# Sums of exponentials of two head groups: from TensorE products with ones to GpSimd additions

## The chip, the cores and the metric

One core of a Trainium2 chip runs the whole program in one launch. The time is the device time of an execution in microseconds (us); the figure for a kernel is the median of its runs. The engines are TensorE (PE), VectorE (DVE), ScalarE (ACT), GpSimd (POOL), and SyncE (SP), whose queue issues most transfers.

## The reference

Two layers over x of 8 x 112 x 512 with a context of 8 x 375 x 512: an attention without projections, a feed-forward with ternary weights, a second attention with projections, and a last feed-forward with integer weights. The change lies in the second attention, which is, for 16 heads of 32:

```
q = hs @ Wq.T + bq ; k = ctx @ Wk.T + bk ; v = ctx @ Wv.T + bv
scores = clip(q k^T / sqrt(32), -50, 50), -10000 where masked, clipped again to -50
probs  = softmax(scores) over the 375 context tokens
delta  = clip(residual_scale, 0, 0.3) * ((probs @ v) @ Wo.T + bo)
x      = x + layernorm(delta) * gamma + beta
```

The softmax is computed as exp(score) and a division by the sum over tokens afterwards. This sum, one number per element, head and query row, is what the change computes in another way.

## The kernel before

The program is written by hand for each engine, with semaphores; no scheduler moves anything, so each engine works in the order in which the code of its block stands.

Stages in order of time: first attention with the key and value projections of the context beside it (to about 135 us), ternary feed-forward (to about 240 us), query projection (to about 266 us), second attention (266 to 370 us), last feed-forward (to the end).

The second attention runs over 8 batch elements (`b`) and in each over G = 4 groups of 4 heads (`g`); m = 4b + g. The context of 375 tokens, padded to 384, lies in TC = 3 chunks of 128 tokens on the partitions. For each m:

- `scores(m)` on PE (L1474): per chunk 4 products, keys as weights, giving 128 tokens x 4 heads x 112 rows in one of four PSUM banks. It runs two groups ahead of the use.
- `exps(m)` on ACT (L1202): three exponentials of 128x448 into `e[g]`, one per chunk, with the mask as bias. There is one buffer `e` per group, so group g of the next element waits until PE has read it (`pv_sum`).
- `clip(m)` on DVE (L1870): one instruction over all three chunks, 128x1344, bounds e to exp(-50) and exp(50). It releases `e_ready`.
- `values(b, g)` on PE: per chunk 4 products of e with the values (L1491), side by side in four column strips of 32, and 4 products of e with `z_pick` (L1494), a tile of ones that puts the sum over the tokens into a row of its own for each group and head. For the last chunk `z_pick_last` has zeros for the tokens beyond 375. The sums of all four groups are gathered in one PSUM bank from the first product of group 0 to the last of group 3.

When group 3 is done, ACT copies the unscaled result (`sums_copy`, L1208), DVE inverts the sums (`invert`, L1876), PE spreads the inverses over the head dimension (`spread`, L1503), DVE multiplies (`normalize`, L1882), and POOL adds the value bias (`value_bias`, L615). PE's order for an element below 4 is scores, spread of the element before, values, and then scores and values in turn.

From element 4 on, the rest of the layer for a tile of 128 rows is woven in: PE runs `project` (L652, 12 products with wo) and `spread` ahead of the element's scores, and from element 5 `normalized_turn` (L660). DVE has `delta_variance` (L671 to L676), `turned_low` (L698), `x3_statistics` (L682 to L689) and `x3_shift` (L694) between the clips. POOL has `delta_inverse` (L620), `x3_inverse` (L624, L626) and, in elements 3 to 6, two conversions of integer weights (L611). In element 2 ACT and in element 3 DVE (L1925) split wo, which the first `project` needs.

DVE's order in one element is: invert(b-1), clip of group 1, context_low, normalize(b-1), delta_variance, turned_low, clip of group 2, x3_statistics, clip of group 3, x3_shift, clip of group 0 of the next element.

SP loads keys (L239, four transfers of 384 KB for an element) and values (L244) two elements ahead, as PE finishes the scores (`s_sum`) and the values (`pv_sum`) of the element that holds the buffers.

Of the kernel before, what the change touches and what calls it, by code (L numbers as in the profile page):

```python
# [21 lines left out]
F32 = mybir.dt.float32  # L22
# [4 lines left out]
ALU = mybir.AluOpType  # L27
# [3 lines left out]
P = 128  # L31
B, S, D = 8, 112, 512
T, TP = 375, 384
TC = TP // P
# [7 lines left out]
G = NH // 4  # L42
# [8 lines left out]
def build(nc, x_in, ctx_tok, ctx_feat, mask_row, mask_tok, w1, w2, w3, wq, wk, wv, wo, bq, bk, bv, bo,  # L51
          gamma, beta, res_scale, wg, sg, wu, su, wd, sd, out):
    with ExitStack() as ctx:
        base = (nc.sbuf_base + 63) // 64 * 64

        def at(name, shape, dtype, offset):
            return nc.alloc_sbuf_tensor_at(name, shape, dtype, offset=base + offset, align_bytes=4)

        def sem(name):
            return ctx.enter_context(nc.semaphore(name))  # L60
# [25 lines left out]
        psum = ctx.enter_context(nc.psum_tensor("psum", [P, 8, 512], F32))  # L86
        psum_bf = psum[:].bitcast(BF16)

        def after(eng, signal, count):

            if not isinstance(count, int) or count > 0:
                eng.wait_ge(signal, count)
# [42 lines left out]
        k_spilled = [sem(f"k_spilled{g}") for g in range(G)]  # L135
# [219 lines left out]
        def move(sp, b):  # L355
            sp.wait_ge(x1_ready, b + 1)
            for _, s, n, k in (r for r in runs if r[0] == b):
                sp.dma_start(xres[n % P:n % P + k, n // P, :], x[s:s + k, b, :]).then_inc(x1_moved[b >= ELEMENTS[0]], 16)
# [153 lines left out]
        z_pick = at("z_pick", [P, G, HD], F32, 190720)  # L512
        z_pick_last = at("z_pick_last", [P, G, HD], F32, 190720 + 512)
# [28 lines left out]

        e = [at(f"e{r}", [P, TC, 4 * S], F32, 56576 + r * 5376) for r in range(4)]
        rz = at("rz", [P, S], F32, 78080)
        ctxt = at("ctxt", [P, KC, N], F32, 198400)
        ctxt_p = [at(f"ctxt_p{q}", [P, 2, KC, P], F32R, 160000 + q * 4096) for q in range(2)]
        y = [at(f"y{q}", [P, D], F32, 168192 + q * 2048) for q in range(2)]
# [8 lines left out]
        s_sum = sem("s_sum")  # L556
        e_raw = sem("e_raw")
        e_ready = sem("e_ready")
        pv_sum = sem("pv_sum")
        ctxt_scaled = sem("ctxt_scaled")  # L560
        z_inv = sem("z_inv")
# [27 lines left out]
        D_UZ = ((6, 7), (4, 5), (6, 7), (4, 5), (4, 5), (4, 5), (4, 5), (4, 5))  # L589
# [15 lines left out]
        def integers(pool, n):  # L605

            if n == 0:
                for pair in range(2):
                    pool.wait_ge(q_stacked[1][pair], STACK)
            pool.wait_ge(wi_loaded[n % 2], 16 * (n // 2 + 1))  # L610
            pool.tensor_scalar(block_of((wg_b, wu_b)[n % 2], n), w_int[n % 2][:], -ZERO_POINT, 1.0, ALU.add, ALU.mult).then_inc(wi_ready, 1)  # L611

        def value_bias(pool, b):
            pool.wait_ge(ctxt_scaled, b + 1)
            pool.tensor_tensor(ctxt[:, :, b * S:(b + 1) * S], ctxt[:, :, b * S:(b + 1) * S],  # L615
                               bqk[:, 2, :].rearrange("p (k o) -> p k o", o=1).to_broadcast([P, KC, S]), ALU.add).then_inc(ctxt_ready, 1)

        def delta_inverse(pool, t):
            pool.wait_ge(y_var, t + 1)
            pool.tensor_tensor(estat[:, 1, t], estat[:, 0, t], neg_half[:, 0:1], ALU.pow).then_inc(y_rstd, 1)  # L620

        def x3_inverse(pool, t):
            pool.wait_ge(x3_mv, t + 1)
            pool.tensor_scalar(rstd[:, t], ln_mv[:, t, 1:2], LN_EPS, 1.0, ALU.add, ALU.mult).then_inc(x3_var, 1)  # L624
            pool.wait_ge(x3_var, t + 1)
            pool.tensor_tensor(rstd[:, t], rstd[:, t], neg_half[:, 0:1], ALU.pow).then_inc(x3_rstd, 1)  # L626
# [296 lines left out]
        def _(pool):  # L923
# [69 lines left out]
            for t in range(TILES):  # L993
                pool.wait_ge(c_xn, t + 1)
                pool.tensor_tensor(xres[:, t, :], xres[:, t, :], rows3[:, 2, :], ALU.add).then_inc(beta_added, 1)

            for b in range(B):
                if b:
                    value_bias(pool, b - 1)
                if b >= 4:  # L1000
                    delta_inverse(pool, b - 4)
                if b >= 4:
                    x3_inverse(pool, b - 4)
                if 3 <= b < 7:
                    integers(pool, 2 * b - 6)
                    integers(pool, 2 * b - 5)
# [14 lines left out]
        def _(act):  # L1021
# [174 lines left out]
            def exps(m):  # L1196

                b, g = m // G, m % G
                after(act, pv_sum, m - 3)
                for c in range(TC):  # L1200
                    act.wait_ge(s_sum, TC * m + c + 1)
                    act.activation(e[g][:, c, :], psum[:, D_S + (TC * g + c) % 4, 0:4 * S], ACT.Exp,  # L1202
                                   bias=mask_bias[:, b, c:c + 1]).then_inc(e_raw, 1)
# [7 lines left out]
            query_hi(1, 0)  # L1211
            query_hi(1, 1)
            exps(0)
            query_hi(1, 2)
            exps(1)
            query_hi(1, 3)
            for b in range(B):
# [72 lines left out]
        def _(pe):  # L1290
# [187 lines left out]
            def values(b, g):  # L1478


                pe.wait_ge(e_ready, G * b + g + 1)
                if g == 0:
                    pe.wait_ge(vst_loaded[b % 2], 16 * (b // 2 + 1))
                    if b < 2:
                        pe.wait_ge(ones_set, 6)
                        pe.wait_ge(q_lo, G + 2 * (b + 1))
                    after(pe, ctxt_scaled, UZ_BEFORE[b] + 1 if UZ_BEFORE[b] is not None else 0)
                for c in range(TC):
                    ends = dict(start=c == 0, stop=c == TC - 1)
                    for hh in range(4):  # L1490
                        mm = pe.matmul(psum[32 * hh:32 * hh + 32, D_UZ[b][0], g * S:(g + 1) * S],  # L1491
                                       vst[b % 2][:, c, (4 * g + hh) * HD:(4 * g + hh + 1) * HD], e[g][:, c, hh * S:(hh + 1) * S], **ends)
                    for hh in range(4):
                        mm = pe.matmul(psum[32 * hh:32 * hh + 32, D_UZ[b][1], 0:S],  # L1494
                                       (z_pick_last if c == TC - 1 else z_pick)[:, g, :], e[g][:, c, hh * S:(hh + 1) * S],
                                       start=(g, c) == (0, 0), stop=(g, c) == (G - 1, TC - 1))
                mm.then_inc(pv_sum, 1)

            def spread(b):
# [79 lines left out]
            with pe.Fori(0, 2) as a:  # L1579
                for m in range(KC):  # L1580
# [3 lines left out]
                    for j in range(JC):  # L1584
                        for u in range(2):
                            mm = pe.matmul(psum[:, F_D + m, 0:HALF], wd_r[:, j, m * P:(m + 1) * P], h_p[:, a, u, j, :],  # L1586
                                           start=(j, u) == (0, 0), stop=(j, u) == (JC - 1, 1))
# [454 lines left out]
```

## Time and profile before

| | us |
|---|---|
| median of 3 runs | 487.19 |
| lowest, highest | 485.66, 490.10 |
| profiled execution, its own time | 488.89 |
| its span | 487.2 |
| PE busy | 467.1 (96% of the span) |
| PE weight loads busy | 355.4 (73%) |
| DVE busy | 294.4 (60%) |
| ACT busy | 235.4 (48%) |
| POOL busy | 83.3 (17%) |

The span runs from the first to the last instruction of the profiled execution; its own time is the device time of the same execution. PE overlaps weight loads and products, so both can be busy at once. "Idle before" in a row is the time that the engine stood still just before it, with what ended the wait; "issue" there is a wait with no cause that the profile shows.

### The profile page before, as it was taken

How to read it: one execution, taken by the hardware profiler on the slowest of the kernel's cores; microseconds unless marked ns; L12 is line 12 of the kernel's file. 1: busy time of each engine (PE TensorE's matmuls, PEld its weight loads, DVE VectorE, ACT ScalarE, POOL GpSimd, SP SyncE). 2: the span in 40 equal slices, each digit the busy share in tenths (PEclk: the TensorE clock that was granted, in tenths of full speed). 3: DMA queues.
4: the chain of work that ended last, by engine and by line, in shares of the span. 5: the costliest groups of instructions: out<-in, count | busy, mean ns of one | idle time of the engine just before them, and what ended most of it. 6: DMA issues, size and time to landing. Idle time of an engine off the chain costs nothing.

```text
span 487.2 us, 10104 instructions
## 1 busy us (share of the span) xinstructions
PE 467.1 (96%) x3942; PEld 355.4 (73%) x3951; DVE 294.4 (60%) x557; ACT 235.4 (48%) x362; POOL 83.3 (17%) x105
## 2 busy tenths in 40 slices
PE   8999999999999899999999688989999999999997
PEld 6877788777877566676798566878886665556996
DVE  4964464458857887655755323777885976555111
ACT  4655433553576365463846545957755492222000
POOL 2210400005024000001071011232332252000000
PEclk9999999999999999999999988999999999999999
DMA  8999787923694145233397977867323452000111
GB/s 274 352 337 358 288 286 237 314 87 126 229 293 132 54 112 149 70 90 77 104 303 216 267 230 283 245 234 240 110 59 119 131 170 68 1 0 0 39 57 57
DMA packets 59181, 82.75 MB, mean 170 GB/s; under 512 B 20097, under 2 KB 43649, under 8 KB 57985
## 3 DMA queue, kind: packets, MB, share of 16 engines
q1 hardware_dynamic: 59136, 82.14, 53.5%
q8 instruction: 30, 0.49, 0.4%
q14 instruction: 13, 0.11, 0.1%
q10 hardware_dynamic: 2, 0.01, 0.0%
HBM read 58.76 MB, written 14.42 MB: 150 GB/s over the span
## 4 chain that ended last, share of the span: by engine, by line
PE 88%; DVE 7%; issue 3%; DMA 1%; ACT 1%; POOL 0%; DVEq 0%; ACTq 0%
PE psum L1536 14%; PE psum L189 13%; PE psum L187 13%; PE psum L1586 7%; PE psum L1377 6%; PE psum L1339 4%; PE psum L652 4%; PE psum L1444 4%; PE psum L1491 4%; PE psum L1322 4%; PE psum L1386 3%; PE psum L1494 3%; PE psum L1474 3%; PE psum L1503 2%; DVE e L1870 1%
## 5 line engine op out<-in xcount | busy, mean ns | idle before, releaser
L189 PE MATMUL psum<-wv_p,kv_p 128*128 128x512 f32 x288 | 76.2, 413 | 0.0
L187 PE MATMUL psum<-kv_p,wk_p 128*128 128x384 f32 x384 | 74.2, 343 | 0.0
L187 PEld LDWEIGHTS psum<-kv_p,wk_p 128*128 128x128 f32 x384 | 66.8, 188 | 2.1 <-issue 0.2
L189 PEld LDWEIGHTS psum<-wv_p,kv_p 128*128 128x128 f32 x288 | 53.7, 188 | 15.8 <-issue 3.7
L1202 ACT ACTIVATE e<-psum,mask_bias 128x448 f32<-128x448 f32 x96 | 53.9, 637 | 22.7 <-PE psum L1474 22.4
L1870 DVE TENSOR_SCALAR e<-e 128x1344 f32<-128x1344 f32 x32 | 28.8, 900 | 20.1 <-ACT e L1202 20.1
L1491 PE MATMUL psum<-e,vst 128*32 128x112 f32 x768 | 38.2, 270 | 1.6 <-issue 0.9
L1536 PE MATMUL psum<-xt,wg_b 128*128 128x448 f16 x176 | 36.9, 352 | 0.3 <-issue 0.3
L1536 PE MATMUL psum<-xt,wu_b 128*128 128x448 f16 x176 | 36.9, 352 | 0.0
L1586 PE MATMUL psum<-h_p,wd_r 128*128 x176 | 36.7, 369 | 0.0
L209 DVE SCALAR_TENSOR_TENSOR khl<-psum,bqk,khl 128x384 f16<-128x384 f32 x32 | 19.6, 613 | 27.0 <-ACT khl L199 26.8
L1586 PEld LDWEIGHTS psum<-h_p,wd_r 128*128 128x128 f32 x176 | 33.0, 188 | 3.4
L1242 ACT ACTIVATE gated<-psum,gs 128x448 f32<-128x448 f32 x22 | 13.9, 633 | 39.4 <-PE psum L1536 33.5
L203 ACT ACTIVATE vsp<-psum 128x512 f32<-128x512 f32 x24 | 14.2, 592 | 31.9 <-PE psum L189 31.9
L1474 PE MATMUL psum<-qst,kst 128*128 128x112 f16 x384 | 25.3, 215 | 4.3 <-issue 4.2
L333 POOL TENSOR_SCALAR w_stage<-w_stage,w_stat 128x2816 f32<-128x2816 f32 x6 | 15.8, 2630 | 79.5 <-DVE w_stat L328 79.4
L1536 PEld LDWEIGHTS psum<-xt,wu_b 128*128 (+1 forms) x176 | 17.2, 98 | 16.1
L1536 PEld LDWEIGHTS psum<-xt,wg_b 128*128 (+1 forms) x176 | 17.1, 98 | 15.6 <-issue 0.7
L199 ACT ACTIVATE khl<-psum,bqk 128x384 f16<-128x384 f32 x32 | 18.3, 576 | 19.6 <-PE psum L187 19.3
L1474 PEld LDWEIGHTS psum<-qst,kst 128*128 128x128 f16 x384 | 20.2, 99 | 9.8 <-issue 8.5
L1936 DVE SCALAR_TENSOR_TENSOR hf<-psum,sgu,gated 128x448 f32<-128x448 f32 x22 | 15.0, 681 | 20.2 <-ACT gated L1242 20.2
L1494 PE MATMUL psum<-e,z_pick 128*32 128x112 f32 x512 | 24.8, 266 | 0.0
(188 smaller groups left out, 815.8 us busy)
## 6 DMA issues: line engine op xcount, KB each, us to landing
kst<-k_scratch SPq DMA_DIRECT2D x32, 384.0 KB, 6.4
kv_raw<-in_ctx_feat SPq DMA_DIRECT2D x12, 768.0 KB, 5.8
w_stage<-in_w SPq DMA_DIRECT2D x6, 1408.0 KB, 8.0
cn<-in_ctx_tok SPq DMA_DIRECT2D x8, 768.0 KB, 9.6
k_scratch<-khl SPq DMA_DIRECT2D x128, 48.0 KB, 1.9
v_scratch<-vsp SPq DMA_DIRECT2D x24, 256.0 KB, 2.8
vst<-v_scratch SPq DMA_DIRECT2D x8, 768.0 KB, 4.6
qst<-qhl SPq DMA_DIRECT2D x32, 112.0 KB, 4.7
```

Source lines behind the costliest of these rows:

```text
L187: mm = pe.matmul(psum[:, kv_bank(p), 0:TP], wk_p[:, u, k, n * P:(n + 1) * P], src[:, v, k, :], **ends)
L189: mm = pe.matmul(psum[:, kv_bank(p), :], src[:, u, k, n * P:(n + 1) * P], wv_p[:, v, k, :], **ends)
L209: dve.scalar_tensor_tensor(khl[n][:, 1, :], psum[:, kv_bank(p), 0:TP], bqk[:, 1, n:n + 1], khl[n][:, 0, :], ALU.add, ALU.subtract).then_in ...
L652: mm = pe.matmul(psum[:, E_O, :], ctxt_p[t % 2][:, u, k, :], wo_p[:, v, k, :], start=(k, u, v) == (0, 0, 0), stop=(k, u, v) == (KC - 1, *P ...
L1202: act.activation(e[g][:, c, :], psum[:, D_S + (TC * g + c) % 4, 0:4 * S], ACT.Exp, bias=mask_bias[:, b, c:c + 1]).then_inc(e_raw, 1)
L1377: mm = pe.matmul(psum[:, B_GU + 2 * ((q + c) % 2) + n, 0:hi - lo], xqt[q][:, k, :], w[:, k, lo:hi], start=k == 0, stop=k == KC - 1)
L1474: mm = pe.matmul(psum[:, D_S + (TC * g + c) % 4, hh * S:(hh + 1) * S], kst[b % 2][:, g, hh, c * P:(c + 1) * P], qst[b // 4][:, hh, g, b % ...
L1491: mm = pe.matmul(psum[32 * hh:32 * hh + 32, D_UZ[b][0], g * S:(g + 1) * S], vst[b % 2][:, c, (4 * g + hh) * HD:(4 * g + hh + 1) * HD], e[g ...
L1494: mm = pe.matmul(psum[32 * hh:32 * hh + 32, D_UZ[b][1], 0:S], (z_pick_last if c == TC - 1 else z_pick)[:, g, :], e[g][:, c, hh * S:(hh + 1 ...
L1536: mm = pe.matmul(psum[:, F_GU + 2 * q + m, 0:HALF], w[:, k, bass.ts(j, P)], xt[:, u, k, a * HALF:(a + 1) * HALF], start=(k, u) == (0, 0), ...
L1586: mm = pe.matmul(psum[:, F_D + m, 0:HALF], wd_r[:, j, m * P:(m + 1) * P], h_p[:, a, u, j, :], start=(j, u) == (0, 0), stop=(j, u) == (JC - ...
L1870: dve.tensor_scalar(e[g][:], e[g][:], EXP_LOW, EXP_HIGH, ALU.max, ALU.min).then_inc(e_ready, 1)
```

## The change

For groups 0 and 1 of each element PE no longer multiplies e by ones. POOL adds the three chunks of e[g] into a tile `zs[g]` of 128x448 with two additions in `fold(b, g)`: chunk 0 plus chunk 1, then chunk 2 on 119 of the partitions, which leaves out the tokens beyond 375. Behind the products of group 3, PE multiplies the two sums by `z_pick`. In `FOLDED` stands the pair (0, 1) for each of the 8 elements.

On POOL, `fold(b, 0)` stands at the start of an element, ahead of value_bias, and `fold(b, 1)` behind delta_inverse and ahead of x3_inverse and the integer conversions. Each fold waits for the clip of its group and until PE has read zs of the element before. PE's group 3 waits for all four additions. ACT's exponentials of groups 0 and 1 wait, from element 1 on, for the additions of the element before, which read the same e. The tiles zs lie where `khl` lay, hence POOL's wait for `k_spilled`.

```diff
+        zs = [at(f"zs{g}", [P, 4 * S], F32, where) for g, where in enumerate((194304, 194304 + 1792))]
+        FOLDED = [(0, 1)] * B
...
+            def fold(b, g):
+                pool.wait_ge(e_ready, G * b + g + 1)
+                after(pool, pv_sum, G * b)
+                pool.tensor_tensor(zs[g][:], e[g][:, 0, :], e[g][:, 1, :], ALU.add).then_inc(z_added, 1)
+                pool.wait_ge(z_added, 4 * b + 2 * g + 1)
+                pool.tensor_tensor(zs[g][0:T - 2 * P], zs[g][0:T - 2 * P], e[g][0:T - 2 * P, 2, :], ALU.add).then_inc(z_added, 1)
+
+            for g in range(G):
+                pool.wait_ge(k_spilled[g], 64 * B)
             for b in range(B):
+                fold(b, 0)
                 if b:
                     value_bias(pool, b - 1)
                 if b >= 4:
                     delta_inverse(pool, b - 4)
+                fold(b, 1)
                 if b >= 4:
                     x3_inverse(pool, b - 4)
...
                 after(act, pv_sum, m - 3)
+                if b and g < 2:
+                    act.wait_ge(z_added, 4 * (b - 1) + 2 * g + 2)
...
-                    for hh in range(4):
-                        mm = pe.matmul(psum[32 * hh:32 * hh + 32, D_UZ[b][1], 0:S],
-                                       (z_pick_last if c == TC - 1 else z_pick)[:, g, :], e[g][:, c, hh * S:(hh + 1) * S],
-                                       start=(g, c) == (0, 0), stop=(g, c) == (G - 1, TC - 1))
+                    if g not in FOLDED[b]:
+                        for hh in range(4):
+                            mm = pe.matmul(psum[32 * hh:32 * hh + 32, D_UZ[b][1], 0:S],
+                                           (z_pick_last if c == TC - 1 else z_pick)[:, g, :], e[g][:, c, hh * S:(hh + 1) * S],
+                                           start=(g, c) == (len(FOLDED[b]), 0), stop=False)
+                if g == G - 1:
+                    pe.wait_ge(z_added, 4 * (b + 1))
+                    for r in FOLDED[b]:
+                        for hh in range(4):
+                            mm = pe.matmul(psum[32 * hh:32 * hh + 32, D_UZ[b][1], 0:S], z_pick[:, r, :], zs[r][:, hh * S:(hh + 1) * S],
+                                           start=False, stop=r == FOLDED[b][-1])
```

In the order of instructions, PE at group 3 of an element. `e_138` is e of group 3, `vst_82` the values, `zs_140` and `zs_141` the new sums. Before:

```order
409 L1491 MATMUL psum<-e_138,vst_82 32x112 [waits e_ready]
410 L1491 MATMUL psum<-e_138,vst_82 32x112 x3
411 L1494 MATMUL psum<-e_138,z_pick 32x112 x4
412 L1491 MATMUL psum<-e_138,vst_82 32x112 x4
413 L1494 MATMUL psum<-e_138,z_pick 32x112 x4
414 L1491 MATMUL psum<-e_138,vst_82 32x112 x4
415 L1494 MATMUL psum<-e_138,z_pick_last 32x112 x4
416 L1474 MATMUL psum<-qst_124,kst_81 128x112 [waits e_raw]
```

And with the change, at the same place, where line numbers are 16 or 17 higher:

```order
399 L1507 MATMUL psum<-e_138,vst_82 32x112 [waits e_ready]
400 L1507 MATMUL psum<-e_138,vst_82 32x112 x3
401 L1511 MATMUL psum<-e_138,z_pick 32x112 x4
402 L1507 MATMUL psum<-e_138,vst_82 32x112 x4
403 L1511 MATMUL psum<-e_138,z_pick 32x112 x4
404 L1507 MATMUL psum<-e_138,vst_82 32x112 x4
405 L1511 MATMUL psum<-e_138,z_pick_last 32x112 x4
406 L1518 MATMUL psum<-zs_140,z_pick 32x112 [waits z_added]
407 L1518 MATMUL psum<-zs_140,z_pick 32x112 x3
408 L1518 MATMUL psum<-zs_141,z_pick 32x112 x4
409 L1490 MATMUL psum<-qst_124,kst_81 128x112 [waits e_raw]
```

Eight products stand behind the 24 of group 3. In groups 0 and 1, twelve products with the values are left in one piece.

POOL in one element from 4 to 6, before (`ctxt` is the context result, `wg_b` and `wu_b` the converted weights):

```order
57 L615 TENSOR_TENSOR ctxt<-ctxt,bqk 128x4x112 [waits ctxt_scaled]
58 L620 TENSOR_TENSOR estat<-estat,neg_half 128x1 [waits y_var]
59 L624 TENSOR_SCALAR rstd<-ln_mv 128x1 [waits x3_mv]
60 L626 TENSOR_TENSOR rstd<-rstd,neg_half 128x1 [waits x3_var]
61 L611 TENSOR_SCALAR wg_b<-w_int_151 128x4x128 [waits wi_loaded0]
62 L611 TENSOR_SCALAR wu_b<-w_int_152 128x4x128 [waits wi_loaded1]
```

And with the change (`e_135` and `e_136` are e of groups 0 and 1):

```order
79 L1003 TENSOR_TENSOR zs_140<-e_135 128x448 [waits pv_sum,e_ready]
80 L1005 TENSOR_TENSOR zs_140<-zs_140,e_135 119x448 [waits z_added]
81 L618 TENSOR_TENSOR ctxt<-ctxt,bqk 128x4x112 [waits ctxt_scaled]
82 L623 TENSOR_TENSOR estat<-estat,neg_half 128x1 [waits y_var]
83 L1003 TENSOR_TENSOR zs_141<-e_136 128x448 [waits pv_sum,e_ready]
84 L1005 TENSOR_TENSOR zs_141<-zs_141,e_136 119x448 [waits z_added]
85 L627 TENSOR_SCALAR rstd<-ln_mv 128x1 [waits x3_mv]
86 L629 TENSOR_TENSOR rstd<-rstd,neg_half 128x1 [waits x3_var]
87 L614 TENSOR_SCALAR wg_b<-w_int_153 128x4x128 [waits wi_loaded0]
88 L614 TENSOR_SCALAR wu_b<-w_int_154 128x4x128 [waits wi_loaded1]
```

Two additions stand ahead of value_bias and two ahead of x3_inverse. The order on DVE, ACT and SP is unchanged.

## Rows read from the trace of the kernel before

**Rows 1.** The page's chain that ended last: shares of the span by engine.

```profile
PE 88%; DVE 7%; issue 3%; DMA 1%; ACT 1%; POOL 0%; DVEq 0%; ACTq 0%
```

**Rows 2.** Stretches, elements 1, 3, 4, 6: length, busy per engine, clock, DMA share, GB/s.

```profile
core 0: us, PE busy (x) PEld busy (x) DVE busy (x) ACT busy (x) POOL busy (x), PEclk, DMA share, GB/s
279.00:292.30 13.30, 10.71 (x248) 9.15 (x245) 4.42 (x6) 6.86 (x13) 1.48 (x1) 0.87 0.79 230
...
305.40:315.20 9.80, 9.25 (x248) 7.80 (x249) 7.94 (x8) 9.49 (x17) 2.70 (x3) 1.00 0.88 276
315.20:329.40 14.20, 11.83 (x260) 10.18 (x260) 10.41 (x18) 7.56 (x14) 4.78 (x6) 1.00 0.65 220
...
341.70:354.10 12.40, 12.25 (x271) 10.57 (x265) 10.35 (x19) 8.95 (x17) 5.04 (x8) 1.00 0.36 110
```

**Rows 3.** PE timeline, element 6, group 3 and on: start, length, engine, line, instruction, idle before.

```profile
352.78 0.40 PE L1491 MATMUL psum<-e,vst 128*32 128x112 f32 x8 [0.15 <-DVE e L1870]
353.00 0.38 PE L1494 MATMUL psum<-e,z_pick 128*32 128x112 f32 x8
353.19 0.38 PE L1491 MATMUL psum<-e,vst 128*32 128x112 f32 x8
...
354.07 3.03 PE L652 MATMUL psum<-wk_p,ctxt_p 128*128 128x512 f32 x12
356.94 1.04 PE L1503 MATMUL psum<-rz,z_spread 128*128 128x112 f32 x8
```

**Rows 4.** DVE timeline, element 6, from normalize to the clip of group 3.

```profile
345.69 0.62 DVE L1882 TENSOR_TENSOR ctxt<-ctxt,psum 128x448 f32<-128x448 f32 x1 [1.13 <-PE psum L1503]
...
349.28 0.85 DVE L1870 TENSOR_SCALAR e<-e 128x1344 f32<-128x1344 f32 x1
...
350.29 0.75 DVE L685 SCALAR_TENSOR_TENSOR xres<-y,estat,xres 128x512 f32<-128x512 f32 x1
...
351.90 0.83 DVE L1870 TENSOR_SCALAR e<-e 128x1344 f32<-128x1344 f32 x1
```

**Rows 5.** Waits 266 to 370 us: line, releaser: total, times, longest.

```profile
PE psum L1494 <- issue: 5.2, 2, 2.9
PE psum L1474 <- issue: 4.2, 2, 2.1
...
PE psum L1491 <- issue: 0.9, 1, 0.9
```

**Rows 6.** PE timeline at two of these breaks, and spread after the first.

```profile
278.32 0.38 PE L1494 MATMUL psum<-e,z_pick_last 128*32 128x112 f32 x2 [2.89 <-issue]
...
279.65 2.05 PE L1503 MATMUL psum<-rz,z_spread 128*128 128x112 f32 x8 [0.25 <-DVE rz L1876]
...
299.98 1.00 PE L1474 MATMUL psum<-qst,kst 128*128 128x112 f16 x9 [2.08 <-issue]
```

**Rows 7.** POOL and DVE timelines where the two run side by side.

```profile
309.58 0.94 POOL L615 TENSOR_TENSOR ctxt<-ctxt,bqk 128x448 f32<-128x448 f32 x1 [12.98 <-DVE ctxt L1882]
309.85 1.38 DVE L1870 TENSOR_SCALAR e<-e 128x1344 f32<-128x1344 f32 x1 [0.35 <-ACT e L1202]
...
348.18 0.99 POOL L620 TENSOR_TENSOR estat<-estat,neg_half 128x1 f32<-128x1 f32 x1 [0.85 <-DVE estat L675]
...
370.90 0.68 DVE L665 TENSOR_TENSOR ctxt_p<-ctxt,ctxt_p 128x512 fp32r<-128x512 f32 x1
371.06 1.31 POOL L615 TENSOR_TENSOR ctxt<-ctxt,bqk 128x448 f32<-128x448 f32 x1 [5.32 <-DVE ctxt L1882]
```

**Rows 8.** DVE and PE timelines at the end of element 3.

```profile
311.43 1.08 DVE L1870 TENSOR_SCALAR e<-e 128x1344 f32<-128x1344 f32 x1 [0.20 <-ACT e L1202]
312.44 2.69 DVE L1925 TENSOR_TENSOR wk_p<-wk_raw,wk_p 128x2048 fp32r<-128x2048 f32 x1
...
315.23 2.99 PE L652 MATMUL psum<-wk_p,ctxt_p 128*128 128x512 f32 x12 [0.25 <-issue]
```

**Rows 9.** PE timeline, element 7, the first products of group 2.

```profile
362.51 0.40 PE L1491 MATMUL psum<-e,vst 128*32 128x112 f32 x8 [0.24 <-DVE e L1870]
```

**Rows 10.** DMA queues, 268 to 330 us: packets, MB, share of 16 engines.

```profile
q1 hardware_dynamic: 7041, 15.15, 78.6%
q8 instruction: 10, 0.16, 1.1%
```

More of the change, by code:

```diff
@@ L558, in build @@
         e_ready = sem("e_ready")
+        z_added = sem("z_added")
         pv_sum = sem("pv_sum")
```

## The prediction

> **What bounds the kernel now.** I read the page's chain first: TensorE (PE) is 88% of what ended last, VectorE (DVE) 7%, "issue" 3% [rows 1]. A share over 487 us says little of a stage of 100 us, so the second view is the table of stretches, cut at the start of each element of the second attention (266 to 367 us) [rows 2]. The reader is to see that the elements are not alike. In element 1 (279.0 to 292.3) PE is busy 10.71 of 13.30 us and DVE only 4.42. In element 6 (341.7 to 354.1) PE has 12.25 of 12.40 and DVE 10.35: both are full. So a faster PE can be worth something in the first elements, and in the last ones only if DVE keeps up.
>
> Third, PE's timeline through one group [rows 3]. A `values` step is sets of four products side by side, eight MATMUL records each; sets start 0.19 us apart (353.00, 353.19). The step of six sets runs from 352.78 to 354.07, 1.29 us. The first set of this group began after an idle 0.15 us that ended with DVE's clip of e. Fourth, DVE over the same element [rows 4]: it starts at 345.69 with the product that needs `spread`, and works with hardly a gap until the clip of group 3 ends at 351.90 + 0.83 = 352.73. PE starts that group at 352.78. So in elements 5 and 6 the loop that sets the time is: project (354.07, 3.03), spread (356.94), DVE's 7.04 us, the last `values` (1.29), and round again. PE's groups 0 to 2 lie beside DVE's work, not on that loop.
>
> Fifth, the breaks called "issue" between 266 and 370 us: 5.2 + 4.2 + 0.9 = 10.3 us in five breaks [rows 5]. They come in the middle of products that wait for nothing (an idle 2.89 before 278.32, 2.08 before 299.98), and `spread` took 2.05 us at 279.65 [rows 6] where it takes 1.04 elsewhere [rows 3]: PE's clock was at 1.2 GHz after the pause. The granted clock of that stretch is 0.87 [rows 2], which is 0.13 x 13.3 = 1.7 us lost. What I take to be behind the breaks is the instruction queue: 10 packets of 16 KB between 268 and 330 us, beside bulk queues that fill most of 16 engines [rows 10]; their times fit the breaks, but that is a reading, no measured cause.
>
> **What the change takes from PE.** Per element it drops 24 products with ones (groups 0 and 1) and adds 8 behind group 3: six sets out, two in. That is 0.19 x 3 = 0.57 us less in group 0 and in group 1, and 0.19 x 2 = 0.38 more in group 3: 0.76 less per element, 6.1 us over eight elements if PE were the limit throughout.
>
> **Elements 0 to 2.** DVE has half its time free, the clips come early, and PE gets its 0.76 each: 3 x -0.76 = -2.3. If ScalarE's exponentials become the limit in the short groups this is nearer 0. I take -2.3.
>
> **Element 3.** `project` starts at 315.23, right after DVE has split wo (312.44 + 2.69 = 315.13), and DVE's clip before it began only when ScalarE had finished [rows 8]. PE's gain ends there in a wait, so it is 0. On top come POOL's additions, which now stand ahead of its integer conversions. POOL's nearest row is the add of 128x448 at 309.58, 0.94 us [rows 7]; two additions are 1.9 us. The bounds are 0 (DVE passes them) and +1.9 (both stand in its way); I take +0.9.
>
> **Element 4.** It holds one of the breaks, and PE sets its end with DVE busy 10.41 of 14.20 [rows 2]. So -0.76; at worst 0.
>
> **Elements 5 and 6.** The 0.57 of groups 0 and 1 are worth nothing, since group 3 still waits for DVE. The two sets behind group 3 are on the loop: +0.38. Then POOL against DVE. POOL's pow ends at 348.18 + 0.99 = 349.17 [rows 7], the additions for group 1 stand right behind it, and DVE's clip of group 2 starts at 349.28 [rows 4]. What a clip loses beside a POOL add is a row: 1.38 us at 309.85 beside POOL's 0.94 at 309.58, against 0.85 at 349.28 [rows 4, 7]; it loses 0.53. It ended 0.71 after POOL did, so beside an addition from 349.25 to 350.19 it would end at 350.90 instead of 350.13: 0.77 at most, 0 if it comes first. I take 0.53. Behind it DVE has an instruction with two SBUF inputs (350.29, 0.75). No row shows such a one delayed by POOL; the nearest is the reverse, POOL's add taking 1.31 instead of 0.94 at 371.06 beside DVE's two-input subtraction at 370.90 [rows 7]. Bounds 0 and 0.75; I take that row's 0.37. The sum is 0.38 + 0.53 + 0.37 = 1.28 each, +2.6.
>
> The Trainium skill ("SBUF — State Buffer", section "Who interferes with whom") speaks against this change: a DVE instruction with two SBUF inputs contends with a GpSimd instruction that reads SBUF, and whichever comes second waits for the whole of the other. With a full block of both instructions, elements 5 and 6 would come to about 1.9 us each by that rule; the trace agrees in the one direction that it shows.
>
> **Element 7.** `values` of group 2 waits 0.24 us for the clip [rows 9], so the clip's 0.53 goes through; the clip of group 3 has project(4) as cover. With the two sets, +0.9.
>
> **Waits that are added.** PE's wait for `z_added` stands behind all of group 3; POOL's additions for group 1 run from about 349.3 to 351.5, the wait is at 354: nothing. ScalarE's exponentials of the next element's groups 0 and 1 wait for the additions that read the same e. Behind them stand the clips of the next element, which DVE reaches more than a microsecond later: nothing, at most 0.5. Behind POOL's additions stand `value_bias` (needed two steps later) and `x3_inverse`, which comes free at about 352: nothing while two additions take under 2.5 us. SP's loads wait for pv_sum and s_sum as before.
>
> **PE's instruction stream.** 16 products fewer in each of 8 elements are 512 fewer records (each is two MATMULs and two weight loads, as the eight records of a set of four show). If a break comes where a piece of program is asked for while the key loads of the next element fill the queues, they come about once per element whatever the length of the stream, so I expect the same number in other places: 0. The ends are one break more or less, 2.9 us and up to 1.7 of slow clock: 4.6 either way.
>
> **Sum.** -2.3 + 0.9 - 0.76 + 2.6 + 0.9 = +1.3. The profiled execution took 488.89 us (span 487.2), so such a one would take 490.2. It stands 1.7 over the median 487.19, and by the median the forecast is 488.5, +0.3%. A measurement of this kernel tells about 1% from no change, 4.9 us.
>
> **Rivals.** (1) PE is the limit all through, and what waits in elements 3 to 7 follows it: 6.1 us less, 481. For it: PE 88% of the chain [rows 1]. Against it: groups that start on a clip [rows 3, 9] and a project that starts on the wo split [rows 8]. Chance 0.10. (2) POOL blocks DVE fully wherever they meet: element 3 +1.9, elements 5 and 6 0.38 + 0.77 + 0.75 = 1.9 each, element 7 0.38 + 0.77 = 1.15, less 2.3 and 0.76: +3.8, 491.0, slower. It decides as soon as DVE's loop of 7.04 us [rows 4] grows by more than the 0.15 us that PE idles. For it: the clip of 1.38 and the add of 1.31 [rows 7]. Against it: it needs POOL to be first each time, by a margin of 0.1 us. Chance 0.22. (3) The shorter stream shifts the pieces so that one break goes, 488.5 - 4.6 = 484, or one comes, 493: 0.12 and 0.08. (4) The change does not do what it says, because ScalarE waits for POOL and PE's shorter groups only wait for exponentials: elements 0 to 2 give 0, which is 490.8. Chance 0.08. The forecast's own case has 0.40.
>
> The range is 483.0 to 493.5: it holds all of these but the first and the tails of the third. Faster by over 1% (under 482.3) is rival 1 and a little of 3: 0.12. Slower by over 1% (over 492.1) is the upper part of 2 and of 3: 0.18. Within 1%: 0.70.
>
> **What would show it.** In the changed profile: PE busy about 6 us less, the products with ones on e half as many, with 64 on the new sums; elements 0 to 2 shorter by 0.8 each unless a break moves; elements 5 and 6 longer by about 1.3, with a longer PE wait for the clip of group 3, and clips of 1.2 to 1.6 us beside POOL's additions; DVE's two-input instructions at 0.75 or at 1.1 and more decide between the forecast and rival 2. The five breaks: count and sum. I am wrong if elements 5 and 6 get shorter (DVE was no limit) or if an addition takes well over 1 us, so that POOL delays `x3_inverse` and with it the loop.

## The result and the profile after

With the change 490.25 us (median of 22 runs, 487.04 to 493.04), before 487.87 us (22 runs, 483.25 to 491.51); ratio 1.0061, 95% interval 1.0040 to 1.0083. The kernel is 0.6% slower, about 3 us; by the two medians it is 2.4 us. A ratio compares the fast executions of both kernels alone, so it can differ from the ratio of the medians. The profiled execution took 490.70 us with a span of 489.0, 1.8 us more than the one before.

The chain that ended last, of the page of the changed kernel, answers to [rows 1]:

```profile
PE 80%; DVE 10%; POOL 4%; DMA 3%; issue 3%; ACT 0%; SPq 0%; POOLq 0%; DVEq 0%
```

POOL had 0% of the chain before and has 4% now. The table of stretches, cut at elements 3 to 6 (length, busy time of each engine with its count, clock, DMA share, GB/s), answers to [rows 2]:

```profile
301.20:312.40 11.20, 8.64 (x214) 6.96 (x212) 10.93 (x8) 7.10 (x14) 9.80 (x6) 0.97 0.76 262
312.40:326.40 14.00, 12.33 (x232) 10.28 (x228) 11.97 (x17) 9.10 (x17) 10.57 (x12) 0.90 0.64 209
326.40:340.80 14.40, 11.76 (x236) 9.83 (x232) 13.48 (x19) 8.91 (x17) 10.47 (x11) 1.00 0.58 203
340.80:355.20 14.40, 11.76 (x237) 9.84 (x233) 13.48 (x19) 8.88 (x17) 10.47 (x11) 1.00 0.31 93
```

In elements 5 and 6 (the last two rows) PE now idles 2.6 of 14.4 us, and DVE is busy 13.48 where it was 10.35 in 12.4. No instruction was added on DVE: the 3.1 us more are the same instructions taking longer.

PE's timeline in element 6, groups 2 and 3 (start, length, line, instruction, idle before), answers to [rows 3]:

```profile
350.29 0.40 PE L1507 MATMUL psum<-e,vst 128*32 128x112 f32 x8 [1.46 <-DVE e L1893]
...
353.52 0.40 PE L1507 MATMUL psum<-e,vst 128*32 128x112 f32 x8 [1.18 <-DVE e L1893]
...
354.70 0.57 PE L1518 MATMUL psum<-zs,z_pick 128*32 128x112 f32 x16
355.19 3.01 PE L655 MATMUL psum<-wk_p,ctxt_p 128*128 128x512 f32 x12
358.05 1.04 PE L1526 MATMUL psum<-rz,z_spread 128*128 128x112 f32 x8
```

Both groups wait for a clip, 1.46 and 1.18 us where it was 0 and 0.15. DVE's timeline through the same element, with POOL's additions among it, answers to [rows 4, 7]:

```profile
341.61 1.16 POOL L1003 TENSOR_TENSOR zs<-e 128x448 f32<-128x448 f32 x1
...
341.86 1.63 DVE L1893 TENSOR_SCALAR e<-e 128x1344 f32<-128x1344 f32 x1
...
342.85 1.63 POOL L1005 TENSOR_TENSOR zs<-zs,e 119x448 f32<-119x448 f32 x1
...
343.41 1.62 DVE L668 TENSOR_TENSOR ctxt_p<-ctxt,ctxt_p 128x512 fp32r<-128x512 f32 x1
...
344.95 0.61 DVE L1905 TENSOR_TENSOR ctxt<-ctxt,psum 128x448 f32<-128x448 f32 x1
...
348.39 1.12 POOL L1003 TENSOR_TENSOR zs<-e 128x448 f32<-128x448 f32 x1
...
348.53 1.70 DVE L1893 TENSOR_SCALAR e<-e 128x1344 f32<-128x1344 f32 x1
...
349.59 1.63 POOL L1005 TENSOR_TENSOR zs<-zs,e 119x448 f32<-119x448 f32 x1
...
350.39 1.39 DVE L688 SCALAR_TENSOR_TENSOR xres<-y,estat,xres 128x512 f32<-128x512 f32 x1
```

Four DVE instructions meet four additions, and each grows. The clip of group 2 takes 1.70 us against 0.85 and ends 0.72 after POOL's addition (348.39 + 1.12 = 349.51, 348.53 + 1.70 = 350.23). The update of xres takes 1.39 against 0.75. The clip of group 1 takes 1.63, and the two-input subtraction (L668) 1.62 where [rows 7] has 0.68. The second addition is itself held by the clip: 1.63 us, where the same form took 1.13 at 280.59 beside an idle DVE. The ends show the two engines taking turns: the clip ends at 343.49, the addition 0.99 us later at 344.48, the subtraction 0.55 us after that at 345.03. DVE's next instruction, L1905, starts with no idle time before it; before, it had waited 1.13 us for `spread` [rows 4].

PE's groups between 266 and 373 us, with busy time and mean, and behind the second bar the idle time before them and what ended it, answer to [rows 5]:

```profile
L1507 PE MATMUL psum<-e,vst 128*32 128x112 f32 x768 | 32.6, 266 | 13.6 <-DVE e L1893 9.1 <-issue 4.3 <-DVE ctxt L1905 0.2
...
L1511 PE MATMUL psum<-e,z_pick 128*32 128x112 f32 x256 | 13.3, 267 | 0.6 <-issue 0.6
...
L1511 PE MATMUL psum<-e,z_pick_last 128*32 128x112 f32 x128 | 7.1, 268 | 1.2 <-issue 1.2
...
L1518 PE MATMUL psum<-zs,z_pick 128*32 128x112 f32 x128 | 5.8, 291 | 2.3 <-POOL zs L1005 2.3
```

The waits called "issue" sum to 4.3 + 0.6 + 1.2 = 6.1 us, where it was 10.3. The last row is PE's wait for POOL, 2.3 us, all of it in element 3. ScalarE waited for POOL too: 6.3 us in three waits. The end of element 3, on POOL, DVE (L1948 is its split of wo), PE and ACT:

```profile
306.61 1.75 POOL L1003 TENSOR_TENSOR zs<-e 128x448 f32<-128x448 f32 x1
...
307.28 3.22 DVE L1948 TENSOR_TENSOR wk_p<-wk_raw,wk_p 128x2048 fp32r<-128x2048 f32 x1
...
308.43 3.06 POOL L1005 TENSOR_TENSOR zs<-zs,e 119x448 f32<-119x448 f32 x1
...
311.54 0.93 PE L1518 MATMUL psum<-zs,z_pick 128*32 128x112 f32 x16 [2.29 <-POOL zs L1005]
311.57 1.68 ACT L1218 ACTIVATE e<-psum,mask_bias 128x448 f32<-128x448 f32 x3 [4.10 <-POOL zs L1005]
...
312.40 4.25 PE L655 MATMUL psum<-wk_p,ctxt_p 128*128 128x512 f32 x12
```

The second addition met the split and took 3.06 us. PE waited 2.29 us for it, and then its `project` took 4.25 us where it took 2.99 before [rows 8]; the granted clock of the stretch that holds it is 0.90.

Elements 0 to 3 are counted from the first product with the values to the first `project`, the others by the start of PE's `project`, element 7 to the first product of the last feed-forward. The two profiled executions divide so:

```
                        before   after   difference
elements 0 to 3          48.3     45.3    -3.0
element 4                14.19    14.01   -0.2
element 5                12.31    14.39   +2.1
element 6                12.34    14.39   +2.05
element 7 and turnover   16.49    17.88   +1.4
rest of the span       383.5    383.0     -0.5
```

The -3.0 is no pure saving. Elements 0 to 3 lost 8.2 us to "issue" before and 6.1 us now; with the change 0.9 us of waiting for the keys and the 2.3 us for POOL came in.

### The profile page after: what moved, and what is told of

It reads as the page before. It is cut to its first block, busy times and chain, and to the rows that moved or that the text cites. A ratio compares the mean times of both kernels' runs of the same rounds, so it can differ in the third digit from the quotient of the medians.

```text
span 489.0 us, 9649 instructions
## 1 busy us (share of the span) xinstructions
PE 461.4 (94%) x3695; PEld 349.0 (71%) x3695; DVE 311.8 (64%) x557; ACT 234.6 (48%) x362; POOL 129.7 (27%) x137
## 3 DMA queue, kind: packets, MB, share of 16 engines
HBM read 58.76 MB, written 14.42 MB: 150 GB/s over the span
## 4 chain that ended last, share of the span: by engine, by line
PE 80%; DVE 10%; POOL 4%; DMA 3%; issue 3%; ACT 0%; SPq 0%; POOLq 0%; DVEq 0%
PE psum L1559 14%; PE psum L189 13%; PE psum L187 13%; PE psum L1609 7%; PE psum L1393 6%; PE psum L1355 4%; PE psum L1460 4%; PE psum L1338 4%; PE psum L1402 3%; PE psum L655 3%; DMA kst<-k_scratch 2%; DVE e L1893 2%; PE psum L1507 2%; PE psum L1490 1%; POOL zs L1005 1%
## 5 line engine op out<-in xcount | busy, mean ns | idle before, releaser
L1218 ACT ACTIVATE e<-psum,mask_bias 128x448 f32<-128x448 f32 x96 | 52.7, 645 | 19.1 <-PE psum L1490 12.8
L1893 DVE TENSOR_SCALAR e<-e 128x1344 f32<-128x1344 f32 x32 | 38.9, 1217 | 11.1 <-ACT e L1218 11.0
L1507 PE MATMUL psum<-e,vst 128*32 128x112 f32 x768 | 32.6, 266 | 13.6 <-DVE e L1893 9.1
L1507 PEld LDWEIGHTS psum<-e,vst 128*32 128x32 f32 x768 | 19.8, 111 | 18.0 <-DVE e L1893 10.3
L1005 POOL TENSOR_TENSOR zs<-zs,e 119x448 f32<-119x448 f32 x16 | 27.0, 1685 | 1.3
```

The source lines that it names most:

```text
L1005: pool.tensor_tensor(zs[g][0:T - 2 * P], zs[g][0:T - 2 * P], e[g][0:T - 2 * P, 2, :], ALU.add).then_inc(z_added, 1)
L1893: dve.tensor_scalar(e[g][:], e[g][:], EXP_LOW, EXP_HIGH, ALU.max, ALU.min).then_inc(e_ready, 1)
```

## The experiments

The median of before beside each group of runs was 488.15, 488.91, 487.03 and 488.12 us. Ratios are to it.

**Fold in elements 0 to 2 only.** The waits on `z_added` count only the groups that are folded.

```diff
-        FOLDED = [(0, 1)] * B
+        FOLDED = [(0, 1)] * 3 + [()] * (B - 3)
```

> Edit: only elements 0 to 2 are folded, elements 3 to 7 are as before the change. Theory (POOL's additions hold up DVE's loop in elements 5 to 7, and the early elements gain): elements 5 and 6 are back at 12.3 us (14.4 with the whole change), the early part keeps what it gained, and the kernel is 1 to 3 us faster than before (ratio 0.994 to 0.998). Rival (the early elements gain nothing, their 2.8 us are only breaks in the instruction stream that fell elsewhere): ratio 1.000 within the noise. Rival (the loss is not in elements 3 to 7): still 1.004 or more.

Measured: 483.30 us, ratio 0.9924 (0.9890 to 0.9959). In the trace the late elements are back: `spread` starts 12.33 us apart. Faster than before and than the change, by a little more than the theory said. That the early elements gain nothing is out, and so is a loss outside elements 3 to 7.

That part of the gain lies in the breaks is not out. From the first product with the values to `spread` in element 3, the four profiled kernels of this document whose PE multiplies all of e by ones there took 36.8 to 39.5 us (mean 38.2), the ten that fold 32.8 to 35.0 us (mean 34.3). Of the 3.9 us between the means, 2.5 us are waits called "issue": 6.9 to 8.5 us in the four, 3.2 to 6.3 us in the ten. The rest, about 1.4 us, holds the sets that PE saves and, in six of the ten, a wait of 0.65 to 1.5 us for the keys. Why the breaks cost less there was not tested.

**POOL's additions alone.** PE multiplies all of e by ones as before and does not read zs.

```diff
-                    if g not in FOLDED[b]:
+                    if True:
...
-                if g == G - 1:
-                    pe.wait_ge(z_added, 4 * (b + 1))
-                    for r in FOLDED[b]:
...
```

> Edit: POOL makes all 32 additions and ACT waits for them as in the change, but PE still multiplies e by ones for all groups and never reads the sums. Theory (the loss is POOL's additions against DVE's clip, its two-input subtraction and its two-input update): elements 5 and 6 last 14.4 - 0.38 = 14.0 us, the clip of group 2 takes 1.7 and the update of xres 1.4 us; elements 0 to 2 gain nothing; the kernel is 5 to 8 us slower than before (ratio 1.010 to 1.016). Rival (the loss is PE's two extra sets behind group 3 and its wait for the sums): elements 5 and 6 stay at 12.3 to 12.6 us and the ratio is 1.000 to 1.003.

Measured: 493.73 us, ratio 1.0141 (1.0088 to 1.0195). DVE's timeline of this kernel in element 5:

```profile
336.37 1.71 DVE L1887 TENSOR_SCALAR e<-e 128x1344 f32<-128x1344 f32 x1
338.01 0.20 DVE L685 TENSOR_SCALAR estat<-estat,rs 128x1 f32<-128x1 f32 x1
338.24 1.39 DVE L688 SCALAR_TENSOR_TENSOR xres<-y,estat,xres 128x512 f32<-128x512 f32 x1
```

The same 1.7 and 1.39 without any change on PE. The spreads of elements 5 and 6 are 13.81 and 14.42 us apart. The second of these is not the 14.0 that was expected: taking PE's two sets away gave nothing there, a first sign that they are not what ends last. (At the start of element 5 DVE still waited for PE, 0.69 and 0.29 us, so the first is no steady element.) So the additions make the loss; PE's new wait does not.

**PE's part alone.** POOL fills zs once and adds nothing.

```diff
-                fold(b, 0)
...
-                fold(b, 1)
...
-                    pe.wait_ge(z_added, 4 * (b + 1))
+                    pe.wait_ge(z_added, 2)
```

> Edit: PE as in the change (groups 0 and 1 without products with ones, two sets behind group 3), but POOL makes no addition; zs is filled once with a constant, so the sums of groups 0 and 1 are left out of the computation. Theory (DVE's loop sets elements 5 and 6 also without POOL's additions): they last 12.33 + 0.38 = 12.7 us, elements 0 to 4 gain 0.76 each where no break moves, and the kernel is 2 to 4 us faster than before (ratio 0.992 to 0.996). Rival (PE was the limit everywhere): elements 5 and 6 at 11.6 us, ratio 0.987 or less.

Measured: 481.68 us, ratio 0.9904 (0.9866 to 0.9942), just under the stated 0.992 and above the rival's 0.987, which its interval just reaches. The trace decides: the spreads of elements 5 and 6 are 12.70 and 12.69 us apart and not the rival's 11.6: +0.37 each, as worked out for the two sets. This run and the one before it add up to 1.0141 + 0.9904 - 1 = 1.0045, near the change's 1.0061. PE's timeline in element 6 shows that DVE is the limit also here:

```profile
341.66 0.40 PE L1498 MATMUL psum<-e,vst 128*32 128x112 f32 x8 [0.41 <-DVE e L1884]
...
344.26 0.40 PE L1498 MATMUL psum<-e,vst 128*32 128x112 f32 x8 [0.54 <-DVE e L1884]
```

PE's shorter groups 0 and 1 become waits before groups 2 and 3.

**PE's two sets ahead of group 3's clip wait.**

```diff
             def values(b, g):
+                if g == G - 1 and FOLDED[b]:
+                    pe.wait_ge(z_added, added(b, G))
+                    for r in FOLDED[b]:
...
                 pe.wait_ge(e_ready, G * b + g + 1)
```

> Edit: as the change, but PE's two sets on the sums stand ahead of its wait for the clip of group 3, beside DVE's work, not behind group 3. Theory (they are on the loop in the change): elements 5 and 6 last 14.39 - 0.38 = 14.0 us and the kernel is 0.4 to 1.5 us faster than with the change (ratio to before 1.002 to 1.005, where the change has 1.006). Rival (PE has slack there too): no difference from the change.

Measured: 493.07 us, ratio 1.0121 (1.0070 to 1.0171). The theory failed: elements 5 and 6 stay at 14.39 us each, from `spread` to `spread`. PE's timeline in element 6:

```profile
353.26 0.59 PE L1507 MATMUL psum<-zs,z_pick 128*32 128x112 f32 x16
...
354.50 0.40 PE L1519 MATMUL psum<-e,vst 128*32 128x112 f32 x8 [0.66 <-DVE e L1899]
```

The sets are out of the way and PE waits for the clip all the same. With the additions in, the loop is no longer DVE, `values`, `project`, `spread` and round: it is DVE alone, which has 13.48 us of work, 0.71 us of wait for POOL's rstd, and no wait for PE. The kernel is also slower than the change, which neither side had expected. In the profiled execution, 2.5 us longer than that of the change, 1.25 us had already come before the second attention began. Inside it one cause shows: in element 7 PE paused 2.39 us for a clip, and then its products ran slowly (0.60 us for a row that takes 0.40; the stretch from 365 to 369 has a granted clock of 0.57, most of it at 1.2 GHz), 1.9 us more in this element than with the change. In element 3, from `spread` to `spread`, it was 0.8 us more. That this happens in each run was not shown.

**Additions of half the length.**

```diff
-                pool.tensor_tensor(zs[g][:], e[g][:, 0, :], e[g][:, 1, :], ALU.add)
+                pool.tensor_tensor(zs[g][:, 0:2 * S], e[g][:, 0, 0:2 * S], e[g][:, 1, 0:2 * S], ALU.add)
```

> Edit: the change with each of POOL's additions over 224 columns instead of 448 (heads 2 and 3 of the sums of groups 0 and 1 hold a constant and are left out of the computation); nothing else differs, not an instruction more or less in the loops. Theory (in elements 5 and 6 DVE works all the time, and the 14.4 us are its own work plus what POOL's additions block): each block falls with the addition's length, the clip of group 2 takes 1.1 to 1.3 us instead of 1.70, the update of xres about 1.0 instead of 1.39, and elements 5 and 6 last 12.9 to 13.5 us; ratio to before 0.995 to 1.002. Rival (what counts is PE's wait for POOL or the number of instructions on POOL, not their length): 14.0 or more.

Measured: 484.80 us, ratio 0.9949 (0.9912 to 0.9986). DVE and POOL in element 6:

```profile
343.23 0.65 POOL L1003 TENSOR_TENSOR zs<-e 128x224 f32<-128x224 f32 x1
...
343.37 1.23 DVE L1895 TENSOR_SCALAR e<-e 128x1344 f32<-128x1344 f32 x1
...
343.96 1.16 POOL L1005 TENSOR_TENSOR zs<-zs,e 119x224 f32<-119x224 f32 x1
...
344.76 0.92 DVE L688 SCALAR_TENSOR_TENSOR xres<-y,estat,xres 128x512 f32<-128x512 f32 x1
```

With 0.65 us of addition the clip takes 1.23 instead of 1.70, the update 0.92 instead of 1.39, and elements 5 and 6 last 13.25 and 13.28 us. The same instructions, waits and products as in the change, only shorter additions, turn a loss into a gain. The length of POOL's additions on DVE's path is the cause.

**Fold in elements 4 to 7 only.**

```diff
-        FOLDED = [(0, 1)] * B
+        FOLDED = [()] * 4 + [(0, 1)] * (B - 4)
```

> Edit: only elements 4 to 7 are folded, elements 0 to 3 are as before the change. Theory (the loss lies wholly in the late elements): 2.05 us more in each of elements 5 and 6, 1.4 in element 7, about 0 in element 4, +5 us, ratio 1.008 to 1.014, and together with the run that folds elements 0 to 2 (0.992) it gives about the change's 1.006. Rival (the early elements' additions cost too, or the two halves depend on each other): below 1.006.

Measured: 494.16 us, ratio 1.0149 (1.0079 to 1.0218, from four executions), just above the stated 1.014, elements 5 and 6 at 14.39 us again. This and the run with elements 0 to 2 add up: 1.0149 + 0.9924 - 1 = 1.0073, the change has 1.0061.

**Fold in elements 0 to 3.**

```diff
-        FOLDED = [(0, 1)] * B
+        FOLDED = [(0, 1)] * 4 + [()] * (B - 4)
```

> Edit: elements 0 to 3 are folded. Element 3 is the one where DVE splits wo and PE waited 2.29 us for POOL's second addition (3.06 us long beside the split). Theory: the split takes 3.2 us again and PE waits about 2 us for the sums in element 3, so this is 0.5 to 2 us slower than folding elements 0 to 2 (ratio 0.994 to 0.998). Rival (the wait only takes up time that PE would have spent waiting for the split): the same as with elements 0 to 2, 0.992.

Measured: 484.21 us, ratio 0.9925 (0.9888 to 0.9962): the rival's number. But both ratios have intervals of 0.35% either way, so a cost of 1 us in element 3 could hide in them, and the trace does not show the rival's mechanism. In element 3 PE did not wait for POOL at all:

```profile
307.81 1.63 POOL L1011 TENSOR_TENSOR zs<-zs,e 119x448 f32<-119x448 f32 x1
...
308.37 3.22 DVE L1954 TENSOR_TENSOR wk_p<-wk_raw,wk_p 128x2048 fp32r<-128x2048 f32 x1
```

Here the second addition started before the split of wo, and took 1.63 us instead of 3.06. What element 3 costs depends on which of the two comes first.

**Elements 0 to 2, with PE's two sets ahead.** Both edits above.

> Edit: elements 0 to 2 are folded, and PE's two sets on the sums stand ahead of the clip wait of group 3. Theory (PE is the limit in these elements, so the place of its two sets does not matter, and POOL is done with its additions long before): within 0.3% of folding elements 0 to 2 with the sets behind group 3 (0.992). Rival (a wait in group 3 there takes up the two sets): 0.6 to 1.2 us faster than that, 0.990.

Measured: 482.31 us, ratio 0.9882 (0.9845 to 0.9920). It looked like the rival, but the intervals overlap and the two kernels had run on different chips, so they were run again side by side (below).

**PE's stream shifted by 64 records.** The kernel before, with work added only at the start.

```diff
             keep_busy(22)
+            for _ in range(32):
+                pe.matmul(psum[:, A_W, 256:264], ones[:, 0:P], ones[:, 0:8], start=True, stop=True)
```

> Edit: the kernel before with 32 more products of 8 columns in PE's warm-up at the very start, 64 records more, where PE waits for x anyway; the second attention is untouched. Theory (PE's breaks are at the ends of pieces of its program of a fixed count of records, and which of them cost time depends on the loads beside them): the breaks between 266 and 370 us stay at the same counts of records from the start (3113, 3367, 3876 and so on, 254 or 255 apart), so 64 records earlier in the code, about a microsecond; their number is 3 to 6 and the time moves by up to 4 us either way without any change in that stage. Rival (the breaks are tied to a place in the code): same products as before, and the time the same within 0.2%.

Measured: 486.36 us, ratio 0.9998 (0.9970 to 1.0026). Counting PE's MATMUL and weight load records from the start of each trace, the pauses over 0.7 us, from the start of one record to the start of the next, stand after these counts. The changed kernel has, besides those below, pauses for DVE, POOL and the keys.

```
before    2858 (1.13 us)  3113 (3.14)  3367 (2.60)  3876 (2.29)  4894 (2.34)
shifted                   3122 (2.65)  3376 (2.92)  3631 (1.08)  4141 (1.24)  4651 (0.87)  5159 (0.73)  5667 (0.85)
changed   2866 (0.83)     3120 (2.00)  3375 (2.79)  3885 (1.50)
```

They lie on one grid of 254 to 255 records (up to 9 records apart between runs, from records missing early in a trace), and not at one place of the code. Which of the crossings cost time is different each time. Two of them in the waits of the shifted kernel:

```profile
280.61 0.28 PE L1496 MATMUL psum<-e,z_pick 128*32 128x112 f32 x1 [2.39 <-issue]
...
289.01 0.40 PE L1496 MATMUL psum<-e,z_pick 128*32 128x112 f32 x2 [2.66 <-issue]
```

A grid that stays put when the program is shifted or changed fits crossings from one piece of PE's program to the next; no run tests this further. That a late load of the piece, held by the key loads, makes a crossing cost time fits the packets [rows 10] but was not tried. The shift moved the breaks and not the median, so this one shift of their places was not worth 4 us.

**Elements 0 to 3, with the two sets ahead.** Both edits above.

> Edit: elements 0 to 3 folded, PE's two sets on the sums ahead of group 3's wait for its clip. Theory (in element 3 the sets wait for POOL in either place, and elsewhere the place does not matter): the ratio is that of elements 0 to 3 folded with the sets behind, 0.992, within 0.3%. Rival (the earlier place is worth 0.4%, as 0.988 against 0.992 for elements 0 to 2 suggests): 0.988 or less.

Measured: 485.94 us, ratio 0.9979 (0.9946 to 1.0013), slower than either theory said. One of its 12 executions took 1624.09 us, for a cause that is not known; it has no part in the ratio. PE's timeline in element 3:

```profile
306.45 0.77 PE L1496 MATMUL psum<-qst,kst 128*128 128x112 f16 x12
...
310.79 0.59 PE L1507 MATMUL psum<-zs,z_pick 128*32 128x112 f32 x16 [3.57 <-POOL zs L1011]
```

POOL's second addition comes late, behind the start of DVE's split of wo, and takes 3.06 us. Ahead of group 3 that wait holds up the whole group, 3.57 us; behind it, in the change, part of it lies beside the group's 24 products and 2.29 us are left. The earlier run with the sets ahead had the same 3.57 us, which fits the 0.8 us more in its element 3.

**The two kernels with elements 0 to 2, on one chip.**

> The kernel that folds elements 0 to 2 once more, beside the one with the two sets ahead, on one chip. Theory (the place of the sets does not matter where PE is the limit): both within 0.2% of each other, near the mean of the two ratios seen, 0.990. Rival (0.992 against 0.988 was real): this one 1 to 2 us slower than the other.

> The kernel that folds elements 0 to 2 with PE's two sets ahead of group 3's wait, once more. Theory: 0.988 to 0.992 and within 0.2% of the other. Rival: 0.988 and 1 to 2 us faster than the other. Either way below 0.995, faster than both the kernel before and the change.

Measured: 483.82 us, ratio 0.9952 (0.9917 to 0.9987), with the sets behind, and 483.60 us, ratio 0.9935 (0.9900 to 0.9970), with the sets ahead: 0.2 us apart. No effect of the place of the sets shows there. Both beat the kernel before and the change in both of their runs; over the four the gain is 0.5 to 1.2% of before. The simple one, which folds elements 0 to 2 and leaves PE's order as the change has it, is the version to keep.

## Why the prediction was right, and where it was not

The forecast was +0.3% and the result +0.6%, inside the range, with the sign of the forecast's sum. The mechanism held: DVE's loop is the limit of the late elements, POOL's additions lengthen it, and the early elements gain. Most sizes were wrong, and the total came close partly by luck, because a larger loss in the late elements and a larger gain in the early ones offset each other.

- Elements 0 to 2, -2.3: the sign is right, and the two runs that fold these alone gave -2.3 and -3.7 us. But the term stood for saved sets only, and in the traces 2.5 of 3.9 us are shorter breaks, which the forecast had put at 0.
- Element 3, +0.9: open by the medians (0.9925 against 0.9924, 0.35% either way). In the profile of the change it cost more: from `spread` to `project` 10.44 us against 8.86, which is about the 2.29 us wait for POOL less 0.76 of sets. It was foreseen as DVE being held up; it fell on PE.
- Element 4, -0.76: measured -0.2. Its break of 2.13 us went. Waits for the clips of groups 2 and 3 (0.24 and 1.22 us) came in its place, since here too DVE took over, and `project` at the slower clock behind the wait for POOL took 1.26 us more. These with the 0.76 of sets make the -0.2; the slow clock was in no term of the sum.
- Elements 5 and 6, +1.28 each: measured +2.08 and +2.05. This is the step that was mis-sized. The parts: the clip of group 2 lost 0.85, not 0.53; the update of xres 0.64, not 0.37. Both are near the bounds that rival 2 took, 0.77 and 0.75, since POOL was first each time. Missed altogether were the additions for group 0, against the clip of group 1 (1.63 for 0.79) and the subtraction L668 (1.62 for 0.67). I had looked only at the additions for group 1. These 1.8 us stand ahead of normalize, where DVE had 1.13 us to spare, so they are not hidden. An addition alone took 1.13 us, and I took 0.94 from a row with another operand.
- The two sets behind group 3, +0.38: right when POOL adds nothing (12.70 and 12.69 us), and worth nothing in the change, because a DVE that never waits for PE hides them. So the 2.05 is not a sum with 0.38 in it. It is DVE's 3.1 us more work less the 1.13 us that it used to wait.
- Element 7, +0.9: +1.4, for the same reason.
- Waits that are added, put at nothing, at most 0.5: right in elements 5 to 7. Wrong for PE's in element 3 (2.29 us), and for ACT's for the additions that read the same e: 0.93 us in element 2, 4.10 in element 3 and 1.27 in element 4. ACT's waits are not shown to be on the path.
- Breaks, 0: they went from 10.3 to 6.1 us in one profile, within the 4.6 stated. That this is chance alone does not fit the traces: over the early elements all ten kernels that fold them lost less to breaks than all four that do not.

Of the rivals, the first (PE the limit all through) is out by the run without additions: elements 5 and 6 got longer with less PE work. The second was the right one in its mechanism, POOL blocking DVE fully, for elements 5 to 7. Its 1.9 us for elements 5 and 6 is near the measured 2.05 partly by luck: it holds the 0.38 of the sets, which was worth nothing, and lacks the group 0 additions. Its total of +3.8 us is nearer to the 3 us of the ratio than the forecast's 1.3. Its chance of 0.22 was too low: the row of the clip at 1.38 us, which ended 0.71 after POOL did, already had the full block in it, and I averaged against a lucky order for which there was no row.

The Trainium skill's rule ("SBUF — State Buffer", section "Who interferes with whom") that a DVE instruction with two SBUF inputs waits for the whole of a GpSimd instruction that reads SBUF, and the other way round, agrees with the traces in both directions now: 0.75 became 1.39 us and 0.67 became 1.62, and POOL's addition of 1.13 became 3.06 behind the start of DVE's two-input split of wo, ending 0.99 us after it. The clip has one SBUF input and is no case of that sentence, but it met POOL in the same way: 0.85 became 1.70, and an addition behind it 1.63.

## What to carry to other kernels

Work moved from PE to POOL is paid on DVE where the two meet: look at which DVE instructions will stand beside every one of the new POOL instructions, not only at those nearest to the critical one, and price each meeting as the whole of the other. Sum DVE's own time per loop before and after, since a loop through several engines can turn into one engine's loop, and then no reordering elsewhere helps. Where stages have different limits, apply such a change to the stages where PE alone is the limit: here three of eight elements, 0.5 to 0.8% faster, where all eight are 0.6% slower. Look also at waits of the engine that is the limit for something that can come late, as PE's for POOL in element 3: it can bring a lower clock behind it.

## What the runs showed of the hardware beyond that

PE's pauses within unbroken products stand at fixed counts of its instruction stream, every 254 to 255 records. A single one cost up to 4.1 us; in the second attention of the 14 kernels profiled the pauses sum to 4.5 to 10.3 us. The Trainium skill ("Runtime: NRT & Kernel Launch", section "Instruction fetch mechanics") has blocks of 256 instructions, which is close to the 254 to 255 records counted here, and calls the cost of a crossing mostly hidden; at most of these counts no pause shows here, but the 4.5 to 10.3 us are not hidden.

After some of these pauses, after the wait of 2.29 us for POOL, and after one of 2.39 us for a clip, PE's products ran at 1.2 GHz for a while, so that a wait of 2 us could cost nearly 4: in element 2 of the kernel before, a pause of 2.08 us and, at a granted clock of 0.87 over 13.1 us, another 1.7 us. After another wait for a clip, 2.32 us long in element 7 of the change, the clock stayed at 2.4 GHz.
